# The adjacency's sigmoid written as a hyperbolic tangent, and the mask turned into a 0/1 tile first

## The reference, cut to what matters

```
sim = einsum('bhnd,bhmd->bnm', Q, K) / (sqrt(d) * H)      # 4 batches of 256 x 256; the divisor is 16
threshold = top_k(sim, 76)[0][:, :, -1:]
A = sigmoid(sim) * (sim >= threshold)
A = (A + swapaxes(A, -1, -2)) * 0.5
gamma = sigmoid(gamma_raw)
x = layernorm(x + (1 - gamma) * x + gamma * A)
```

## Time and profile before

| What | Value |
|---|---|
| Median of 3 runs | 671.9 us (671.45 to 673.34) |
| Span of the profiled execution, first to last instruction | 670.2 us |
| Busy: PE, PE's weight loads, DVE, ACT, POOL | 650.0, 556.9, 519.6, 499.6, 389.0 us |
| Mean granted TensorE clock | 0.999 of full |

### The profile page before, as it was taken

How to read it: one execution, slowest core, us unless ns; L and a number is a source line. 1 busy time by engine, 2 the same in 40 slices (tenths; PEclk the granted TensorE clock), 3 DMA queues, 4 the chain that set the end, 5 groups by cost and what they waited for, 6 DMA issues and landing times.

```text
span 670.2 us, 15648 instructions
## 1 busy us (share of the span) xinstructions
PE 650.0 (97%) x5342; PEld 556.9 (83%) x5342; DVE 519.6 (78%) x1684; ACT 499.6 (75%) x1305; POOL 389.0 (58%) x644
## 2 busy tenths in 40 slices
PE   8999999999999999999999999999999999999996
PEld 5779888998898999789977788889788887778886
DVE  3989998997999998567977955556799888849464
ACT  4888786969678785799888766675768686866653
POOL 3488556556655754689769545464772321525842
PEclk9999999999999999999999999999999999999999
DMA  8642022123213120410031020121020000010401
GB/s 331 190 140 63 18 79 73 48 49 95 54 59 113 40 61 21 111 34 2 1 99 60 0 95 1 48 95 40 8 95 4 3 3 4 3 48 1 141 9 56
DMA packets 27299, 40.20 MB, mean 60 GB/s; under 512 B 3914, under 2 KB 19794, under 8 KB 27220
## 3 DMA queue, kind: packets, MB, share of 16 engines
q1 hardware_dynamic: 26932, 38.74, 18.7%
q10 hardware_dynamic: 288, 0.46, 0.3%
HBM read 29.09 MB, written 1.05 MB: 45 GB/s over the span
## 4 chain that ended last, share of the span: by engine, by line
PE 77%; DVE 7%; POOL 4%; ACT 3%; DMA 3%; issue 3%; SPq 2%; DVEq 0%; POOLq 0%; ACTq 0%
PE bank L1287 67%; PE bank L1301 8%; SPq L2800 2%; PE bank L1593 2%; DMA front_pack<-in_front 1%; DMA qT<-xT_plain 1%; POOL probs L2549 1%; POOL qT L2549 1%; DVE u_pair_lo L2072 1%; POOL w_split_lo L2549 1%; POOL probs L2546 1%; ACT x L1736 1%; DVE g_pair_lo L2072 1%; SPq L2721 1%; DVE bn L2095 1%
## 5 line engine op out<-in xcount | busy, mean ns | idle before, releaser
L2546 POOL TENSOR_SCALAR probs<-probs,soft 128x256 f32<-128x256 f32 (+1 forms) x256 | 104.0, 428 | 54.9 <-DVE soft L2231 53.8
L1840 ACT ACTIVATE probs<-probs,soft 128x256 f32<-128x256 f32 (+1 forms) x256 | 113.1, 445 | 20.0 <-DVE soft L2223 19.6
L2549 POOL TENSOR_TENSOR w_split_lo<-w_raw,w_split_hi 128x512 fp32r<-128x512 f32 (+2 forms) x57 | 76.4, 1352 | 52.0 <-ACT w_split_hi L1729 51.7
L1287 PE MATMUL bank<-xT_hi,w_split_hi 128*128 128x512 f32 x256 | 103.5, 404 | 1.6 <-DVE xT_lo L2072 1.1
L1287 PE MATMUL bank<-xT_lo,w_split_hi 128*128 128x512 f32 x256 | 100.5, 393 | 0.0
L1287 PE MATMUL bank<-xT_hi,w_split_lo 128*128 128x512 f32 x192 | 75.4, 393 | 0.0
L2223 DVE CUSTOM_DVE_ANT_0 probs<-bank,front_pack 128x128 f32<-128x128 f32 (+1 forms) x192 | 58.0, 329 | 17.2 <-PE bank L1287 16.4
L1287 PE MATMUL bank<-keyT,qT 128*64 128x64 f32 (+3 forms) x800 | 63.4, 302 | 2.6 <-POOL qT L2549 1.9
L1287 PEld LDWEIGHTS bank<-keyT,qT 128*64 128x64 f32 x800 | 58.0, 137 | 8.9 <-issue 3.3
L1729 ACT ACTIVATE probsT<-bank 128x384 f32<-128x384 f32 x128 | 53.7, 490 | 14.5 <-PE bank L1301 14.1
L1287 PEld LDWEIGHTS bank<-xT_hi,w_split_hi 128*128 128x128 f32 x256 | 48.1, 188 | 14.1 <-issue 2.4
(11 more groups left out here) (262 smaller groups left out, 1886.2 us busy)
## 6 DMA issues: line engine op xcount, KB each, us to landing
w_raw<-in_w_front SPq DMA_DIRECT2D x8, 768.0 KB, 4.8
w_raw_heads<-in_w_back SPq DMA_DIRECT2D x8, 640.0 KB, 4.5
qT<-xT_plain SPq DMA_DIRECT2D x68, 64.0 KB, 2.0
qT<-rope_buf SPq DMA_DIRECT2D x32, 64.0 KB, 2.0
w_raw<-in_w_gateT SPq DMA_DIRECT2D x8, 256.0 KB, 2.7
w_raw<-in_w_upT SPq DMA_DIRECT2D x8, 256.0 KB, 3.4
w_raw<-in_w_downT SPq DMA_DIRECT2D x8, 256.0 KB, 3.7
w_raw<-in_L_ffn_Wup SPq DMA_DIRECT2D x7, 256.0 KB, 2.7
```

Of the source, the lines that this page charges most:

```text
L1287: return t.matmul(out, lhsT, rhs, start=start, stop=stop, skip_group_check=shared)
L1840: ins = s.activation(p[:, at], p[:, at], ACT.Exp, bias=st[:, 0, r:r + 1], scale=-1.0, accum_out=st[:, 1, r:r + 1])
L2546: return g_.tensor_scalar(out, in0, s1, s2, op0, op1)
L2549: return g_.tensor_tensor(out, in0, in1, op)
```

## The change

ACT computes tanh(score/32) in place of exp(-score/16). With s = score/16, sigmoid(s) = (1 + tanh(s/2))/2. DVE first overwrites the scores with 1 where they reach the threshold and 0 elsewhere, and then computes (tanh + 1) x mask in one instruction. The result is twice the old one, so the column by which `att_mix` multiplies becomes gamma/4. The addition before the reciprocal and the reciprocal are gone. The planner's cost of a mask step goes from 2.7 to 0.95. The mask step now also waits for the last round of `adj_top` on its tile explicitly, as its first instruction reads `best`.

```
         for i in range(TB):
-            stage(("adj_mask", b, i), "DVE 2.7", ("adj_top", b, ROUNDS - 1))
+            stage(("adj_mask", b, i), "DVE 0.95", ("adj_top", b, ROUNDS - 1))
...
-    sim_exp = signal("sim_exp", keys("adj_sim", range(TB)))
+    sim_tanh = signal("sim_tanh", keys("adj_sim", range(TB)))
...
                     w.wait_ge(*sim_copied[b, i])
-                    s.activation(sim_buf[i][:, 2, :], sim_buf[i][:, 0, :], ACT.Exp, scale=-1.0 / 16).then_inc(sim_exp.sem, 1)
+                    s.activation(sim_buf[i][:, 2, :], sim_buf[i][:, 0, :], ACT.Tanh, scale=1.0 / 32).then_inc(sim_tanh.sem, 1)
...
-                own(ts(gate_col[:, 2:3], gate_col[:, 1:2], 0.5, None, ALU.mult))
+                own(ts(gate_col[:, 2:3], gate_col[:, 1:2], 0.25, None, ALU.mult))
...
             elif name == "adj_mask":
                 b, i = k
-                sim, sig, at = sim_buf[i][:, 0, :], sim_buf[i][:, 2, :], (TOPK - 1) % 8
-                w.wait_ge(*sim_exp[b, i])
-                own(ts(sig, sig, 1.0, None, ALU.add))
+                sim, twice, at = sim_buf[i][:, 0, :], sim_buf[i][:, 2, :], (TOPK - 1) % 8
+                w.wait_ge(*sim_tanh[b, i])
+                w.wait_ge(*rows_of_sim[b, i])
+                own(ts(sim, sim, best[i][:, at:at + 1], None, ALU.is_ge))
                 w.wait_ge(*own.now)
-                own(v.reciprocal(sig, sig))
-                w.wait_ge(*own.now)
-                stt(adjacency[:, TB * b + i, :], sim, best[i][:, at:at + 1], sig, ALU.is_ge,
-                    ALU.mult).then_inc(adj_masked.sem, 1)
+                stt(adjacency[:, TB * b + i, :], twice, 1.0, sim, ALU.add, ALU.mult).then_inc(adj_masked.sem, 1)
```

## The result

The changed kernel takes 674.1 us (median of 16 runs) against 672.6 us before, a ratio of 1.0029 with a 95% interval of 1.0016 to 1.0043 (the ratio of the two medians alone is 1.0022). The profiled execution has a span of 672.6 us against 670.2 us. Single executions of either kernel spread over 3 to 5 us, so ratios over many runs decide here, and profiles, of one execution each, say where the time went.

What follows compares the result with a forecast made beforehand. PE, busy for 650.0 of 670.2 us, was taken as the bound. Its 1.7 us of idleness from 80 to 110 us would go, all other terms zero: 671.9 - 1.7 = 670.2 us, range 668.6 to 673.6 us.

Steps and rivals of the forecast that it cites:

- the three gaps: 80 to 110 us: PE idles 0.7 us for y, 0.2 us for `w_split_hi`, 0.8 us for qT; all go.
- The sum for the arithmetic: Whole kernel: removing reciprocals takes 14.3 us off DVE, 3.6 us in the backlog; PE gains 1.7 us.
- the third gap: PE's 0.8 us wait for POOL's addition to qT; rival that it stays: 671.0 to 671.9 us, chance 0.22.
- The tanh's table and time: ACT's eight tanh: exp's time, within 0.4 us in all, one shared table load; rival unshared: 674.7 us, chance 0.04.
- The second instruction at unchanged cost: Each mask's combined DVE instruction: fastest 0.483 us before, still stretched in places, its cost taken as unchanged.
- the worst case of 2.66 us: First two masks on DVE: both instructions at their maxima, 1.18 + 1.48 us each, eating most of the 3.6 us.
- The planner: Mask cost 2.7 to 0.95: orders may change from the first mask, differences die out by the masks' end, priced at nothing.
- The slower rival: Reordered queues from the first mask on: each miss costs 0.7 to 1.6 us, three give 675.0 us; chance 0.15.
- The gap near 283 us: PE's 1.4 us of idleness from 270 to 285 us, after the last mask; not in the forecast sum.

Runs made afterwards that it cites:

- arith_old_orders: The changed kernel with the planner's mask cost left at 2.7, so the orders and banks of the kernel before; ratio to before 0.9978.
- both_moves: New arithmetic with old orders and banks; on DVE batch 0's second mask directly behind the first, `w_q` 2 behind scores s 1 1 0; ratio to before 1.0008.
- orders_old_arith: The kernel before, old arithmetic, with the planner's mask cost set to 0.95, so the changed kernel's orders and banks; ratio to before 1.0133.

## Why the prediction was wrong, point by point

- *What bounds the kernel, and the three gaps.* Right. The time is decided in these 30 us, PE was fully busy to within 0.2 us from 110 to 270 us, and 7.2 us off DVE's load there (146.96 to 139.78) brought PE forward by nothing: its lag is 1.6 us at 108 us and up to 280 us.
- *The sum for the arithmetic.* Right with the old orders: all 1.69 us of idleness from 80 to 110 us went, forecast -1.7 us, measured -1.5 us (0.9978), and the third gap, for which a rival was set up, closed too. That the numbers agree so well is in part luck, as the trace gives some back at 198 and 282 us. The tanh's table and time were as forecast.
- *The second instruction at unchanged cost.* Off. The mean of the two together went from 1.23 to 1.60 us. I had named the worst case of 2.66 us and set it aside because the first mask would start before POOL's addition. It did; the second mask then ran inside it for 2.85 us. The reciprocal had been time in which POOL got its first addition done without holding DVE. Removing it exposed what stood behind.
- *The planner: the step that failed.* I wrote that I expect "both the backlog and the differences in order to die out by the end of the masks", and priced the new orders at nothing in the sum. They did die out without a trace around the masks of batches 1 and 2. Around those of batch 0 they met the one place where PE waits for DVE: the first masks, the addition to y and `w_q` 2. By the ratios they turned -1.5 us into +2.0 us. My argument held for the 160 us in which the other engines have slack towards PE and not for the 15 us in front of them, although the rows had just shown that PE waited there for exactly these steps. The slower rival had the right mechanism and place ("on DVE a mask or a round of `adj_top` now fits, by the planner, in front of an addition or score that on the chip is the one PE needs, because on the chip masks still stretch beside POOL"), with a chance of 0.15. Its price was 4.8 us for three waits less the 1.7 us recovered, 3.1 us in all; the traces show 1.4 us more idleness from 80 to 110 us and 1.0 us more near 283 us, 2.4 us in all.
- *The scheduler's nature.* The hand-made corrections in `ASIDE`, the planner's table of shifts for single steps, stayed as they were while a cost beside them changed. Each cost is an input to a greedy choice, and a truer one (0.95 for an undisturbed 0.80 us) gave a worse order.
- *The gap near 283 us.* I counted it as beyond the masks. It takes back part of a gain, since the swaps behind 768 KB of loads come earlier by less than PE does: in arith_old_orders PE is there 1.4 us earlier, and POOL, which waits for them, starts on qT 0.7 us earlier (280.08 against 280.80 us). Its size varied between kernels whose orders there are equal (1.1 before, 1.8 in arith_old_orders, 2.1 us after), and how much of this is spread from execution to execution is open. The prediction prices a wait by its length alone; behind the longest of these (2.3 us in both_moves) the granted clock fell and made it dearer.

## What to carry to other kernels

Where a cost also steers a scheduler, change the work and the cost separately, and look at the new order around the instructions that the bounding engine waits for, before pricing the work. An instruction's price in a crowded stretch depends on which neighbours on other engines hold it: a short mask took 1.8 us less than a long one where POOL was idle (0.80 against 2.60 us), and 1.0 us less beside POOL's additions in batch 1 (2.66 against 3.64 us). After a gain, look at the next wait that moves by less than the bounding engine does, here small DMAs behind large loads; it decides how much of the gain reaches the end. And a long wait of PE can cost more than its length: here 3.9 us of waiting came with about 1.5 us of slower work behind it.

## What the runs showed of the hardware that was not expected

- A VectorE instruction of the masks that starts during a GpSimd instruction ends 0.1 to 0.3 us after it: 0.42 us became up to 1.46 us beside an addition of two tensors (1.27 to 1.36 us each pass), and 0.77 us beside one pass of a single tensor (0.62 us).
- A pointer scalar costs a VectorE instruction of 128x256 about 0.06 us (0.338 against 0.273 us for a comparison).
- Three weight loads of 256 KB each (768 KB together) on the same queue in front of swaps of 64 KB made POOL wait 1.5 us for the swaps and PE 1.8 us; behind them, none and 0.4 us.
- Behind a wait of PE of 3.86 us (orders_old_arith) and one of 2.33 us (both_moves) the granted TensorE clock fell to 0.50 (1.2 GHz) for some 3 us, beyond what the wait itself cost; behind waits of 2.09 us (the changed kernel) and 1.77 us (arith_old_orders) it did not.
